# FFN norms of a decoder layer: sums of squares by a 32-column indicator into four partition quarters, instead of by the squares themselves as stationary operand

## The reference

```
x = x + minGRU_both_directions(layernorm(x)) @ W_out + b_out
x = x + cross_attention(layernorm(x), ctx of 1601 rows)
x = x + ffn(layernorm(x))
```

```
q  = batchnorm((h @ Wq + bq).reshape(B, S, 8 heads, 64))
q0 = q[..., :32] / norm(q[..., :32]);  q1 = q[..., 32:] / norm(q[..., 32:])
s0 = q0 . k0;  s1 = q1 . k1            # 32 keys each
the 4 largest of s0, of s1; softmax over their 16 sums; idx = i0*32 + i1
out = sum_k w_k * gelu(expert_down[idx_k] . h) * expert_up[idx_k]
```

## Time and profile before

| | |
|---|---|
| median of 3 runs | 407.18 us (406.18 to 407.36) |
| profiled execution, its time | 404.52 us |
| profiled execution, its span | 402.5 us |
| PE busy | 394.0 us (98%), 2580 instructions |
| PE weight loads busy | 365.1 us (91%) |
| DVE busy | 300.4 us (75%) |
| ACT busy | 237.1 us (59%) |
| POOL busy | 216.1 us (54%) |
| mean granted TensorE clock | 0.996 |

### The profile page before, as it was taken

The page is one execution under the profiler, slowest core; times in us unless marked ns, Lnnn a source line. Parts: engine busy times, 40 slices in busy tenths (PEclk is TensorE's granted clock), DMA queues, the critical chain, the costliest instruction groups (busy, mean ns, idle before and its releaser), DMA issues.

```text
span 402.5 us, 7793 instructions
## 1 busy us (share of the span) xinstructions
PE 394.0 (98%) x2580; PEld 365.1 (91%) x2580; DVE 300.4 (75%) x1093; ACT 237.1 (59%) x519; POOL 216.1 (54%) x209
## 2 busy tenths in 40 slices
PE   8999999999999999999999999999999999999977
PEld 7878888899999999999999999999878998989875
DVE  4798678886756867577774857562786999989996
ACT  3886859454765466354555424352457979688462
POOL 1788999774376323253430210010156869999993
PEclk9999999999999999999999999999999989999999
DMA  7900313004434312224211000000100000000101
GB/s 217 321 3 1 82 54 104 8 1 123 126 107 108 100 45 76 58 68 120 58 53 31 0 2 2 1 2 0 29 1 2 0 2 2 28 29 27 41 28 65
DMA packets 19991, 21.36 MB, mean 53 GB/s; under 512 B 3180, under 2 KB 16624, under 8 KB 19952
## 3 DMA queue, kind: packets, MB, share of 16 engines
q1 hardware_dynamic: 18832, 19.96, 16.6%
q10 hardware_dynamic: 1120, 0.92, 0.8%
HBM read 18.78 MB, written 2.10 MB: 52 GB/s over the span
## 4 chain that ended last, share of the span: by engine, by line
PE 82%; DVE 11%; ACT 4%; issue 1%; POOL 1%; POOLq 0%; DVEq 0%; ACTq 0%
PE keep_pQ L75 11%; PE keep_pQ L76 11%; PE keep_pQ L77 10%; PE context_pA L1051 6%; PE context_pA L1053 6%; PE context_pA L1052 6%; PE context_pR L1085 6%; DVE ffn_top L1649 3%; DVE ffn_picked L1662 3%; PE context_pR L533 3%; PE context_pA L533 3%; PE ffn_pK L1807 2%; PE context_pR L75 2%; PE ffn_pT L1837 2%; PE context_pR L77 2%; PE context_pR L76 2%
## 5 line engine op out<-in xcount | busy, mean ns | idle before, releaser
L899 DVE TENSOR_TENSOR att_pTl<-context_pR,att_pTh 128x512 fp32r<-128x512 f32 x64 | 37.0, 587 | 29.7 <-ACT att_pTh L811 29.4
L811 ACT ACTIVATE att_pTh<-context_pR 128x512 fp32r<-128x512 f32 x64 | 32.1, 514 | 40.0 <-PE context_pR L1085 40.0
L1258 POOL TENSOR_TENSOR ffn_prod<-ffn_first,ffn_near 128x1024 f32<-128x1024 f32 (+1 forms) x29 | 54.2, 1883 | 2.3 <-DVE ffn_first L1687 2.3
L851 ACT ACTIVATE att_prob<-keep_pQ,att_nmax 128x1206 f32<-128x1206 f32 x16 | 20.3, 1269 | 35.9 <-DVE att_nmax L935 35.8
L930 DVE TENSOR_REDUCE att_mx<-keep_pQ 128x1 f32<-128x402 f32 x64 | 34.5, 564 | 6.9 <-PE keep_pQ L77 6.6
L786 POOL TENSOR_TENSOR keep_rstd<-att_ve,keep_mhalf 128x4 f32<-128x4 f32 x3 | 3.0, 1007 | 55.9 <-DVE att_ve L989 55.9
L1085 PE MATMUL context_pR<-keep_ident,att_prob 128*128 128x128 f32 (+1 forms) x208 | 31.8, 273 | 0.2 <-DVE att_pTl L899 0.2
L1837 PEld LDWEIGHTS ffn_pT<-keep_ident,ffn_prod 128*128 128x128 f32 x240 | 26.9, 142 | 5.2 <-DVE ffn_hT L1720 3.2
L1837 PE MATMUL ffn_pT<-keep_ident,ffn_prod 128*128 128x128 f32 x240 | 28.8, 273 | 2.8 <-POOL ffn_prod L1258 2.8
L1051 PE MATMUL context_pA<-att_pTh,context_cNh 128*128 128x256 f32 (+1 forms) x104 | 31.0, 298 | 0.0
L1051 PE MATMUL context_pA<-att_pTh,att_cNh 128*128 128x256 f32 (+1 forms) x104 | 31.0, 298 | 0.0
(11 more groups left out here) (336 smaller groups left out, 1301.1 us busy)
## 6 DMA issues: line engine op xcount, KB each, us to landing
keep_raw<-in_ctxT SPq DMA_DIRECT2D x24, 256.0 KB, 2.7
keep_raw<-in_ctx SPq DMA_DIRECT2D x24, 256.0 KB, 2.9
out<-keep_x SPq DMA_DIRECT2D x16, 128.0 KB, 1.7
keep_x<-in_x SPq DMA_DIRECT2D x3, 512.0 KB, 10.2
gru_wout<-in_W_out SPq DMA_DIRECT2D x1, 512.0 KB, 8.8
keep_raw<-in_fWq SPq DMA_DIRECT2D x2, 256.0 KB
keep_raw<-in_ctxT SPq DMA_DIRECT2D x8, 32.5 KB, 3.1
keep_raw<-in_ctx SPq DMA_DIRECT2D x4, 65.0 KB
```

What stands on the lines that cost most here:

```text
L899: dve.tensor_tensor(to, bank, half(it, 0, n)[0].bitcast(F32), ALU.subtract).then_inc(bank_free, 1)
L1258: return eng.tensor_tensor(prod[:, i % PB, a:b].rearrange("p h (i j) -> p h i j", j=KEYS), (factor if factor is not None else first[:, n % ...
```

## The change

For groups n >= 2 (TILED = 2) the sums of squares are formed the other way round. `group_of` grows to 128 x 32, its columns 4 to 31 zero, and becomes the stationary operand; the 128 x 256 squares of a chunk are the moving one, and chunk c writes partitions 32c to 32c+31 of `pG`, the second half of the bank of `pN` (`column_sums`). ACT copies the 128 x 256 result to `sums` in SBUF (`read_sums`). Then for each of the two tiles PE takes the 128 x 128 of `sums` as stationary and 16 columns of the identity (`picks`) as moving operand, which turns it to token by token in the old place of `pN` (`turned_sums`). `group_of` has 32 columns also in the first two groups' `norms`, which use only 4 of them.

The orders change with it. On PE, `expert_product(6)` and `(7)` go one round earlier, `column_sums(3)` goes to round 1 and `turned_sums(2)` and `(3)` to round 2; from round 4 on `column_sums(n+2)` stands where `norms(n+2)` stood, and `turned_sums(n+2)` behind `mix(i-5)`. On ACT, `read_sums(2)` goes ahead of the loop, `read_sums(3)` behind `exponentials(2)`, the others behind `exponentials(i+1)` of their round; `norm_roots(k)` for k >= 2 moves from ahead of `read_output` and `leftover` to behind them.

```diff
@@ -1148,7 +1148,7 @@
     keysq, keyn, keyT = st.sb("keysq", [P, P]), st.sb("keyn", [P, P]), st.sb("keyT", [P, P])
     k2, ku, kinv = (st.sb(n, [P, 1]) for n in ("k2", "ku", "kinv"))
     pair = st.sb("pair", [P, P])
-    group_of = st.sb("group_of", [P, 4])
+    group_of = st.sb("group_of", [P, HALF])
     ve3 = st.sb("ve3", [P, TPB])
     xn = st.sb("xn", [P, 2, TPB, D])
     q0 = xn[:, 0].rearrange("p t d -> p (t d)").rearrange("p (c n) -> p c n", n=COLS)
@@ -1173,11 +1173,14 @@
     first = st.sb("first", [P, 2, PER, HEADS, FIRSTS])
     prod = st.sb("prod", [P, PB, HEADS, EXPERTS])
     hT = st.sb("hT", [P, 2, DC, P])
+    sums = st.sb("sums", [P, 2, COLS])
 
     pT = pW = st.ps("pT", [P, DC, SEQ])
     pO, pS = pQ[:, 0:2], pQ[:, 2:4]
     pK = pN = st.ps("pK", [P, SEQ])
     pB = st.ps("pB", [P, SEQ])
+    pG = pK[:, COLS:2 * COLS]
+    picks = ident[:].rearrange("p (c g) -> p c g", g=HALF)[:, :, 0:4]
     ny = pB[:, 128:128 + MOST]
     total = pB[:, 256:256 + PER * HALVES].rearrange("p (h s) -> p h s", s=2)
     inv = pB[:, 320:320 + PER * HALVES].rearrange("p (h s) -> p h s", s=2)
@@ -1209,6 +1212,7 @@
                             "h_ready", "out_mm"))
     y_ready, y_added, stored = st.sem("y_ready"), st.sem("y_added"), st.sem("stored")
     x_high, x_low = st.sem("x_high"), st.sem("x_low")
+    sums_mm, sums_read = st.sem("sums_mm"), st.sem("sums_read")
 
     def wait_output(eng, i):
 
@@ -1218,6 +1222,7 @@
             eng.wait_ge(y_added, i - ADDED + 1)
 
     FIRST_POOL, FIRST_ACT = 2, 4
+    TILED = 2
     LASTS = TILES - PER
     SPLIT = {LASTS - 1: (HEADS // 2, HEADS - 2), LASTS: (HEADS - 5, HEADS - 4), LASTS + 1: (HEADS - 5, HEADS - 4)}
     EARLY_GELU = 4
@@ -1419,7 +1424,9 @@
                     .then_inc(q_ready_act, 1)
 
         def squared(n):
-            if n >= 2:
+            if n >= 2 + TILED:
+                act.wait_ge(sums_mm, n - 2 - TILED + 1)
+            elif n >= 2:
                 act.wait_ge(norm_mm, n - 1)
             else:
                 act.wait_ge(bn_ready, 1)
@@ -1432,6 +1439,13 @@
                     act.activation(sq[:, 0, c], q, ACT.Square, scale=bn[:, 0:1], bias=bn[:, 1:2])\
                         .then_inc(sq_ready, 1)
 
+        def read_sums(n):
+
+            act.wait_ge(sums_mm, n - TILED + 1)
+            if n >= TILED + 2:
+                act.wait_ge(norm_mm, n - 1)
+            act.activation(sums[:, n % 2], pG, ACT.Copy).then_inc(sums_read, 1)
+
         def norm_roots(k):
             act.wait_ge(n2_ready, k + 1)
             m = len(BATCHES[k]) * PER * HALVES
@@ -1482,20 +1496,21 @@
         norm_roots(1)
         squared(2)
         squared(3)
+        read_sums(TILED)
         for i in range(TILES):
             n, t = i // PER, i % PER
             if 2 <= i + 1 < TILES:
                 exponentials(i + 1)
+            if i == 1:
+                read_sums(TILED + 1)
+            if t == 0 and i >= 2 * PER and n + 2 < GROUPS:
+                read_sums(n + 2)
             if i == 1:
                 for m in range(EARLY_GELU, EARLY_GELU + DC):
                     expert_raw(m)
             if i == SUM:
                 for m in range(EARLY_GELU + DC, ES):
                     expert_raw(m)
-            if t == 0:
-                for k in range(2, len(BATCHES)):
-                    if n + 2 == BATCHES[k][-1]:
-                        norm_roots(k)
             if t == 1 and FIRST_ACT <= n + 3 < GROUPS:
                 normed(n + 3)
                 squared(n + 3)
@@ -1508,6 +1523,10 @@
             if t == 0 and n >= 1:
                 for j in range(1 if n == 1 else i - PER, i):
                     leftover(j)
+            if t == 0:
+                for k in range(2, len(BATCHES)):
+                    if n + 2 == BATCHES[k][-1]:
+                        norm_roots(k)
             if i == PER * BATCHES[-1][-1] - 2 * PER:
                 for m in range(EARLY_GELU, ES):
                     late_gelu(m)
@@ -1804,7 +1823,28 @@
                 wait_squares(pe, n, c)
                 for t in range(PER):
                     a = (n * PER + t) * HALVES + 4 * c
-                    last = pe.matmul(pN[:, a:a + 4], sq[:, n % 2, c, t * P:(t + 1) * P], group_of[:], start=True, stop=True)
+                    last = pe.matmul(pN[:, a:a + 4], sq[:, n % 2, c, t * P:(t + 1) * P], group_of[:, 0:4], start=True, stop=True)
+            last.then_inc(norm_mm, 1)
+
+        def column_sums(n):
+
+            k = [n in b for b in BATCHES].index(True)
+            if n == BATCHES[k][0]:
+                pe.wait_ge(n2_ready, k)
+            if n > TILED:
+                pe.wait_ge(sums_read, n - TILED)
+            for c in range(QC):
+                wait_squares(pe, n, c)
+                last = pe.matmul(pG[c * HALF:(c + 1) * HALF], group_of[:], sq[:, n % 2, c], start=True, stop=True)
+            last.then_inc(sums_mm, 1)
+
+        def turned_sums(n):
+
+            pe.wait_ge(sums_read, BATCHES[2][-1] - TILED + 1 if n in BATCHES[2] else n - TILED + 1)
+            for t in range(PER):
+                a = (n * PER + t) * HALVES
+                last = pe.matmul(pN[:, a:a + HALVES].rearrange("p (c g) -> p c g", g=4), sums[:, n % 2, t * P:(t + 1) * P],
+                                 picks, start=True, stop=True)
             last.then_inc(norm_mm, 1)
 
         def scores(i):
@@ -1916,7 +1956,7 @@
         scores(2)
         scores(3)
         expert_product(5)
-        norms(2)
+        column_sums(2)
         pe.wait_ge(ld_up, 16)
         for i in range(TILES):
             n, t = i // PER, i % PER
@@ -1924,12 +1964,19 @@
                 scores(i + 2)
             if i == SUM + 1:
                 dense(9)
-            if t == 0 and 3 <= n + 2 < GROUPS:
-                norms(n + 2)
-            if i in (SUM - 1, SUM):
-                expert_product(EARLY_GELU + DC + i - SUM + 1)
+            if t == 0 and TILED + 2 <= n + 2 < GROUPS:
+                column_sums(n + 2)
+            if i == SUM - 2:
+                expert_product(6)
+                column_sums(3)
+            if i == SUM - 1:
+                turned_sums(2)
+                turned_sums(3)
+                expert_product(7)
             if WEIGH + 1 <= i:
                 mix(i - WEIGH - 1)
+            if t == 0 and TILED + 2 <= n + 2 < GROUPS:
+                turned_sums(n + 2)
             if 0 <= i - SUM:
                 if i == SUM:
                     pe.wait_ge(expert_read, DC)
```

## The result

| | before | changed |
|---|---|---|
| median of 20 runs each | 406.43 us | 408.25 us |
| lowest to highest | 405.09 to 407.61 | 406.07 to 411.06 |
| profiled execution, time and span | 404.52, 402.5 | 406.42, 404.3 |
| PE busy, mean granted clock | 394.0, 0.996 | 389.7, 1.000 |

The ratio is 1.0039 (95% interval 1.0022 to 1.0055): slower by 0.2 to 0.6%, where 0.74% was forecast. (This ratio and those of the experiments are not the quotients of the two medians; here these would give 1.0045.)

A forecast was written before the change was run, and what follows sets the result against it. PE, DVE and POOL were taken as nearly full, with DVE, then POOL, setting the end. Lateness root by root reached +3.0 us: profiled 404.52 to 407.5, median 407.18 to 410.2 us; range 408.0 to 413.6, chance 0.78.

The forecast's parts named there:

- Full overlap, roots still late: Rival: column_sums records overlap fully on PE (0.43 us) but ACT's roots stay late; +1.4 us, 408.6 us, chance 0.16.
- I take 5 x 0.215 = 1.07: PE time in us assumed for the eight column_sums records of a group, between bounds of 0.43 and 1.72.
- Records go in order ... which leaves five slots: On PE, a product's two records cannot overlap, but its second and the next product's first can: five 0.215 us slots.
- my sum: Main case: lateness added root by root through rounds 2 to 10, ending at +3.0 us; chance 0.40.
- What is added on PE: Term for turned_sums (0.45 us) and column_sums (1.07 us): PE pays 1.52 for the 1.78 removed, per group.
- the lower bound: column_sums on PE with products side by side except one product's two records: 2 x 0.215 = 0.43 us.
- What is moved: Term for ACT's norm_roots: table load falls behind read_output and leftovers, so the root comes 2.17 us after mix ends.
- Round 4: Step: head sums on PE start +1.0 us late behind ACT's copy and turned_sums, and DVE waits for them.
- Round 10: Step: root +3.8 us late, but 0.85 no longer stands between root and gelus, so ACT's gelus are +3.0.
- PE is the bound in every pair: Premise of a rival: PE limits every pair of rounds up to 370 us, so less PE work could gain time.
- Faster: Rival: PE gets far enough ahead for timely roots and DVE loses its PE waits; -1.8 us, 405.4 us, chance 0.13.

The follow-up runs named there:

- full_width: Changed kernel with the four column products no longer in separate array parts: 128-column indicator, all accumulating into 128 partitions; ratio to the kernel before 1.0120.
- root_early: Changed kernel with norm_roots(2), (3), (4) back ahead of read_output and the leftovers; ratio to the kernel before 0.9979.
- table_early: Changed kernel plus a one-column square root on ACT behind exponentials(i+1) in rounds 2, 6 and 10, loading the table early; ratio to the kernel before 0.9973.
- move_alone: Kernel before with only norm_roots moved behind read_output and the leftovers, without the new sums; ratio to the kernel before 1.0128.
- order_before: Kernel before, old products kept, with norms(4) and norms(6) put behind sum_heads of rounds 4 and 8; ratio to the kernel before 0.9949.
- before_again: Kernel before, unchanged, a second execution with a profile; 406.37 us.
- new_best: Changed kernel, column_sums(4), (6) behind sum_heads, their turned_sums a round later; ACT in rounds 6, 10: leftovers, read_sums, norm_roots, read_output; ratio to the kernel before 0.9927.

## Why the prediction was right or wrong

The direction and the mechanism of the move were right, the size was not: +3.0 us forecast, 0.39% of 406.4 or 1.6 us measured. (The absolute 410.2 us was 1.95 above the measured 408.25; 0.75 of that comes from the median of 3 runs that I started from, 407.18, where 20 runs give 406.43.) The change in time came out as in the rival *Full overlap, roots still late*, which had +1.4 and 0.16. The term that was mis-sized is that of `column_sums`: **I take 5 x 0.215 = 1.07**, measured 0.57. The step under it that failed is the order of the records ("Records go in order ... which leaves five slots").

| lateness, us | my sum | full-overlap rival | measured |
|---|---|---|---|
| root of round 2 | +0.35 | 0 | 0.0 (327.41, 327.75) |
| head sums of round 4 | +1.0 | +0.6 | +0.7 (337.50, 337.14) |
| root of round 6 | +2.5 | +1.5 | +1.9 (348.37, 346.77) |
| root of round 10 | +3.8 | +2.2 | +2.9 (369.08, 366.52) |
| exponential of tile 12 | +3.0 | +1.4 | +2.2 (374.15, 372.33) |

(The measured column is the difference of the two times with the 0.34 us of offset; it is counted from the profiled execution of before, the median's comparison is below.)

- **What is added on PE.** That the two records of one product do not overlap was right: they start 0.24 us apart (356.09, 356.33). That they are worked off product by product, in a chain of five slots, was wrong: four records start together at 344.23, the other four at 344.47, and the next instruction at 344.80. That is the two slots of the lower bound, 0.43, plus 0.14. With 0.57 and the measured +0.7 of round 4, my sum for the root of round 6 gives +1.7 (346.82 + 0.7 - (1.78 - 0.57) + 2.17 = 348.48), near the +1.9 measured. The Trainium skill, "TensorE: Matmul & The Clock Gate", Part 3 on packing small matmuls, gave an estimated 0.72 for them, nearer than my slots; eight records at the 0.216 us of full_width would be 1.73, three times the 0.57. `turned_sums` took 0.37, not 0.45.
- **What is moved.** Right, and shown by three runs: 2.20 us from `mix` to the root (2.17 forecast), the load behind the Copies, DVE stalled 1.37 us twice ("about 1.5" forecast). root_early and table_early remove the stalls by two different edits and win 0.6 and 0.7% over the change; move_alone makes them without the new sums.
- **Round 4.** Right in kind: PE waits for the copy, DVE's wait rises by 0.70, where +1.0 was forecast.
- **Round 10.** The 0.85 us that ACT wins back for the gelus is there: 2.9 late at the root, 2.2 at the exponential.
- **Against the median.** My sum stood on one execution with the clock fallen where it cost nothing. In the second execution of the kernel before a fall in round 8 costs 1.7 us (2.77 - 1.09). The profiled pair differs by 1.90 us, the ratio by 1.6. So of the 1.4 us between +3.0 and 1.6, the table accounts for 0.8 (+3.0 against +2.2 at the exponential of tile 12); the rest lies in the clock and in how executions differ ahead of the changed part (0.34 us here), and was not split further.
- **PE is the bound in every pair** (in the rival *Faster*) is only half true. order_before shows that the work on PE can stay as it is and 0.5% be won by its order, part of it, as far as the two profiles tell, by where the clock falls. That this is the whole of the 2.0 us was not shown: one profile of order_before and two of before are few.

## What to carry to other kernels

Before an instruction that needs another table of functions is put behind others, ask where the table's load will go: in these traces it stays directly ahead of the instruction, so what was loaded in idle time (343.58, root at 346.77) now comes after the last wait. When a product in the middle of an in-order queue is made cheaper, look first at what it stands in front of: here the head sums of rounds 4 and 8 waited behind sums of squares that nobody needed for two more rounds. And take a second profile of the kernel before, if its runs spread more than the effect: the first one was 2 us below the median, and as far as two profiles tell for a reason that the change touched.

## What the runs showed of the hardware that was not expected

Eight float32 records with a stationary operand of 32 columns and 256 moving ones, in four parts of the array, took 0.57 us: four start together, the other four 0.24 us later. With 128 columns into the same output (full_width) they start 0.216 us apart, one by one. The two records of one product are a slot apart in both.

The mean clock of a run separates the changed kernel's runs without exception (1.000: at most 407.41 us; below: at least 408.17). In the kernel before it tells less: over the 52 runs taken beside the experiments and the single executions, those at 0.996 last 404.47 to 406.54 us and those at 0.987 last 406.07 to 408.00. What a fall costs depends on where it lies: one of 3.4 us at product 6 left DVE busy for 2.54 of 2.70 us, one at the head sums of round 8 went with a wait longer by 1.7 us (before_again), and falls between 384 and 390 us with waits of 0.4 to 0.6 us (before_again, order_before, root_early, new_best).

Falls were seen behind products with 4 moving columns, with 0.55 us of waiting ahead of them in before_again and 2.20 in move_alone, and, in the filler, behind two gaps on PE of 1.68 and 0.81 us in new_best and of 1.47 and 0.81 in full_width. They were not seen behind gaps of 1.69 and 0.81 us at the same place nor behind the 2.10 us ahead of `column_sums(6)` in the first profile of the changed kernel. What decides between executions stays open.
